# All low parts of the second attention on GpSimd, and the norms placed among the rotations

## The reference, cut to what matters

```python
xn = (x - mu) / jnp.sqrt(var + 1e-05) * ln_gamma + ln_beta      # for the attention
qkv = xn @ w_qkv                                                # [2048, 3 * 16 * 64]
qr, kr = (rotate(q), rotate(k))                                 # t1 cos - t2 sin, t2 cos + t1 sin
scores = jnp.einsum('bhid,bhjd->bhij', qr, kr) * scale
probs = jax.nn.softmax(scores, axis=-1)                         # 2048 x 2048 for each of 16 heads
out = jnp.einsum('bhij,bhjd->bhid', probs, v)
```

## Time and profile before

| | |
|---|---|
| median of 3 runs | 3486.61 us (3481.0 to 3489.35) |
| the profiled execution | 3484.36 us, its span 3482.6 us |
| busy in the span | PE 87%, PEld 37%, DVE 83%, ACT 86%, POOL 73% |
| granted TensorE clock | 0.872 of full speed |
| first attention and what precedes it | until 1866 us of the span |
| projection stage | 1866 to 2037 us |
| second attention | 2037 to 3308.4 us |
| output stage | the rest |

### The profile page before, as it was taken

How to read it: one execution, slowest core, us unless ns; L and a number is a source line. 1 busy time by engine, 2 the same in 40 slices (tenths; PEclk the granted TensorE clock), 3 DMA queues, 4 the chain that set the end, 5 groups by cost and what they waited for, 6 DMA issues and landing times. The chain is left out here.

```text
span 3482.6 us, 59948 instructions
## 1 busy us (share of the span) xinstructions
PE 3037.7 (87%) x19523; PEld 1275.8 (37%) x19523; DVE 2877.3 (83%) x4324; ACT 2989.6 (86%) x2783; POOL 2537.8 (73%) x1581
## 2 busy tenths in 40 slices
PE   6888888888888888888887968999898889989899
PEld 4222112221222212222223424555555555555547
DVE  7989999999999999999997968878887777888421
ACT  3999999999999999999996846878888888878942
POOL 5888888888888888888875524767777776767850
PEclk9788777887778777887778979999999999999999
DMA  2000000000000000000001550100000110000000
GB/s 75 6 8 7 7 0 7 7 7 7 0 7 7 7 7 0 7 7 7 3 6 40 198 143 19 32 26 26 25 26 26 44 32 26 26 26 25 20 22 13
DMA packets 59522, 85.32 MB, mean 24 GB/s; under 512 B 10065, under 2 KB 45905, under 8 KB 58961
## 3 DMA queue, kind: packets, MB, share of 16 engines
q1 hardware_dynamic: 59344, 82.93, 8.3%
HBM read 52.31 MB, written 30.54 MB: 24 GB/s over the span
## 5 line engine op out<-in xcount | busy, mean ns | idle before, releaser
L1264 POOL TENSOR_TENSOR lo<-pr,hi 128x1024 f16<-128x1024 f32 x384 | 883.1, 2323 | 396.3 <-ACT hi L1438 391.1
L1325 DVE TENSOR_REDUCE mx<-mx_ps 128x1 f32<-128x512 f32 x1024 | 660.6, 683 | 127.7 <-PE mx_ps L1480 123.9
L1453 ACT ACTIVATE pr<-s_ps 128x1024 f32<-128x1024 f32 x512 | 533.2, 1041 | 243.4 <-PE s_ps L1511 189.2
L1438 ACT ACTIVATE hi<-pr 128x1024 f16<-128x1024 f32 x512 | 549.3, 1074 | 0.0
L1480 PE MATMUL mx_ps<-ka,qa 128*128 128x512 f16 x1024 | 376.6, 397 | 128.4 <-DVE mx L1325 98.7
L722 ACT ACTIVATE wt<-wt 128x2048 f32<-128x2048 f32 x256 | 485.2, 1896 | 0.5
L713 ACT ACTIVATE wt<-wt,theta_bias 128x2048 f32<-128x2048 f32 (+2 forms) x160 | 482.4, 3015 | 3.2 <-DVE wt L563 2.7
L501 POOL TENSOR_TENSOR wt<-base,wt 128x1024 f32<-128x1024 f32 x192 | 455.3, 2371 | 16.0
L501 POOL TENSOR_TENSOR wt<-vb,wt 128x1024 f32<-128x1024 f32 x192 | 455.1, 2370 | 16.0
L1530 PE MATMUL pv_ps<-vh,hi 128*128 128x129 f16 x4096 | 434.5, 223 | 10.2 <-ACT sums L1444 3.9
L1530 PE MATMUL pv_ps<-vh,lo 128*128 128x65 f16 x4096 | 420.2, 195 | 0.0
(11 more groups left out here) (210 smaller groups left out, 5046.0 us busy)
## 6 DMA issues: line engine op xcount, KB each, us to landing
qk<-stg SPq DMA_DIRECT2D x6, 2048.0 KB, 10.6
vh<-v SPq DMA_DIRECT2D x16, 520.0 KB, 3.4
qa<-qk SPq DMA_DIRECT2D x16, 512.0 KB, 3.6
ka<-qk SPq DMA_DIRECT2D x32, 256.0 KB, 4.8
v<-v_st SPq DMA_DIRECT2D x3, 2080.0 KB, 7.9
qst<-parts_dram SPq DMA_DIRECT2D x144, 32.0 KB
kst<-parts_dram SPq DMA_DIRECT2D x144, 32.0 KB
qk<-stg SPq DMA_DIRECT2D x4, 1024.0 KB, 8.5
```

The source lines that it names most:

```text
L1264: eng.tensor_tensor(lo[:, i % NHL, :, :], pr_slot(i), hi[:, i % NHL, :, :], ALU.subtract).then_inc(lo_done, 1)
L1325: eng.tensor_reduce(mx4[:, q // NCH, q % NCH:q % NCH + 1], mx_ps[:, q % 2, :], AX.X, ALU.max)\
L1438: eng.activation(hi[:, i % NHL, :, :], pr_slot(i), ACT.Copy).then_inc(hi_done, 1)
L1453: eng.activation(pr_slot(i), s_ps[:, i % 2, :, :], ACT.Exp, scale=SM).then_inc(exp_done, 1)
```

## The change

In the attention stage the steps whose low part DVE makes go from every fourth to none (`NLV = 0`): POOL makes all 32 low parts of a head, in order, and the waits on `lo_vector` and `lo_gpsimd` are counted accordingly. DVE's two half instructions are gone. In the projection stage POOL's 16 norms no longer stand ahead of the low parts of the rotations; one stands behind the second low part of each block.

```diff
-                for k in range(NT):
-                    eng.tensor_scalar(xn[:, k, :], base[:, k, :], mv[:, k, 0:1], tmp[:, 0, k:k + 1],
-                                      ALU.subtract, ALU.mult).then_inc(xn_ready, 1)
                 for u in range(4 * NT):
...
                     eng.wait_ge(hi_ready, u + 1)
                     eng.tensor_tensor(dst[:, :, 1, :], ra[:, u % 2, :].rearrange("p (h e) -> p h e", h=HB),
                                       dst[:, :, 0, :], ALU.subtract).then_inc(lo_ready, 1)
+                    if b == 1:
+                        eng.tensor_scalar(xn[:, k, :], base[:, k, :], mv[:, k, 0:1], tmp[:, 0, k:k + 1],
+                                          ALU.subtract, ALU.mult).then_inc(xn_ready, 1)
...
-    LV = 4
+    NLV = 0
+    NLG = STEPS - NLV
...
         def on_vector(i):
-            return i % LV == LV - 1
+            return i % STEPS >= NLG
...
+            before = h + 1 + i // STEPS
             if on_vector(i):
-                eng.wait_ge(lo_vector, STEPS // LV * (h + 1) + i // LV + 1)
+                eng.wait_ge(lo_vector, NLV * before + i % STEPS - NLG + 1)
             else:
-                eng.wait_ge(lo_gpsimd, STEPS // LV * (LV - 1) * (h + 1) + i // LV * (LV - 1) + i % LV + 1)
+                eng.wait_ge(lo_gpsimd, NLG * before + i % STEPS + 1)
...
-                        for n_ in range(2):
-                            at = i - LOW - n_
-                            if (at >= 0 or not first) and on_vector(at):
-                                low_half(h, at, n_)
...
                     if last:
-                        for n_ in range(2):
-                            low_half(h, STEPS - 1, n_)
                         take(h, NS - 1)
...
-                eng.sem_inc(lo_vector, STEPS // LV)
-                eng.sem_inc(lo_gpsimd, STEPS - STEPS // LV)
+                eng.sem_inc(lo_gpsimd, NLG)
```

More of the change, by code:

```diff
@@ L1365, in take @@
                        .then_inc(attn_ready, 1)
[L1367 to L1376, removed]
                 def one(g, par, first=False, last=False):
```

## The result

The changed kernel takes 3569.99 us (median of 4 runs, 3558.07 to 3571.11) against 3483.81 of the kernel before on the same chips (4 runs, 3480.99 to 3489.35): a ratio of 1.0238, with a 95% interval of 1.0211 to 1.0264. It is slower by some 85 us; 3572 was forecast. The span of the profiled execution is 3569.3 us, 86.7 more than before.

The account below looks back on a forecast made before the run. PE sets the pace, held up by DVE. Heads 1 to 14 +94, head 0 -12, head 15 +8.4, norms -2.5: +88 on 3484.4 gives 3572 us, own range 3520 to 3610, for 8 in 10 3462 to 3610.

Parts of the forecast that it names:

- The mechanism: Second attention: a two-SBUF-input DVE instruction and a POOL low part exclude each other; multiplication 425 ns to about 2.3 us.
- the waiting one goes first: When POOL's low part ends, the waiting DVE instruction starts before POOL's next; a held addition ends 0.28 us later.
- The takes: Middle heads, steps 4, 12, 20, 28: step 4's take grows from 1.04 to 4.45 us; losses total 12.25 us a head.
- the sum: Time of a middle head: 68 + 12.25 + 3 = 83.25 us against 76.5, +6.75; for 14 heads +94.
- The undisturbed head: A middle head without DVE's half low parts and their waits: 68 us, 8.5 less than now.
- The clock: Middle heads: PE's long stops bring two slow clock stretches a head, about 1.5 us each, 3.0 us together.
- the row of maxima: Step 28: the maxima for the next head come some 1.5 us later, costing 0.5 us a head.
- Head 0: First head of the second attention, making maxima for two heads: -12 us, bounds -5 and -17.
- Head 15: Last head, without maxima: POOL's 69 us exceeds ACT's 61, low part 31 ends later; +8.4 us, bounds +5 and +10.
- The norms: Projection stage: DVE's 2.38 us wait goes, the moved norms are covered by 0.4 us of slack; net -2.5 us.
- the addition alone is held: Rival: the multiplication gets in before POOL's next low part; take 2.7 us, 3468 us in all; chance 0.13.
- takes cost little: Rival: takes hardly delay PE and POOL is the limit, 69.5 us a head, 3380 us; chance 0.08.

Follow-up runs that it names:

- the halves: The changed kernel with every low part of GpSimd split into two instructions of 128x512, without a wait between them: 3563.66 us, ratio 1.0219.
- the measured 98: The kernel before with one more multiplication, its result unused, in each take: 3587.10 us, ratio 1.0289; 98 us more, where 12 was expected.

## Why the prediction was right, point by point

- **The mechanism.** Forecast: the multiplication at about 2.3 us, the addition 1.5 to 2.3, three stops of PE a head at the banks after the takes. Measured: 2155 ns, 1560 ns, 42 waits in 14 heads. By the Trainium skill, SBUF — State Buffer, section "SBUF: two separate sides", whichever of the two starts first has the pair of SBUF ports that they share for its whole instruction, and the other is blocked. In the two timelines of step 20 the trace agrees: 2.13 and 2.11 us in place of 0.40 and 0.42. What follows on the end of that instruction the forecast had from one row: that the waiting one goes first. It held in the changed kernel and is false beside the halves (9.7 us).
- **The takes.** Forecast at step 4: 4.45 us; measured over the middle heads 3.82, at steps 12 and 20 3.95 and 4.47. The loss at step 20 is 3.95 us where the sum had 4.1. At step 4 my arithmetic had low part 3 begin on time; POOL comes out of the short steps with a backlog (ten low parts without a gap from 2155.88 us on), which moves its phase against the take, and the addition's hold varies there between 0.5 and 2.4 us in length.
- **The undisturbed head.** 68 us was too high. By the sum's own rule (a take's length less 0.4 is lost) the kernel without the division loses 1.3 + 1.8 + 1.8 = 4.9 in takes of 1.71, 2.17 and 2.21 us, so its 70.9 leave 66. This is an estimate: PE's waits at the banks in that kernel are 3.6 us a head, by which it would be 67.
- **The clock.** Two slow stretches of 1.5 us, 3.0 in all, was too low. By the same rule the takes lose 3.4 + 3.55 + 4.05 = 11.0; 66 + 11 leaves 5.7 of 82.7. One is the row of maxima: PE's wait for it is 25.4 / 14 = 1.8 us a head, where the 0.5 stood. The other 4 or so belong to the clock: 11.6 us of each head ran at half speed, against 1 in the kernel without the division. There were 37 slow stretches in 14 heads, 2.6 a head where I had taken two; 4 us are then 1.5 for each, as forecast. This is a remainder, not a measurement: no run changed the clock alone. What the sum had too high (2.0 in the undisturbed head, 0.75 in the takes) and too low (1.3 in the row, 0.9 in the clock) met, and the head came out at +6.2 against +6.75. That 3572 is within 3 us of 3570 owes something to this.
- **Head 0**: -9.4 against -12; the multiplication slipped in at two of its three takes (0.42 and 0.43 us) and was held at the third (2.23). **Head 15**: +6.4 against +8.4; low part 31 ended 7.7 us later after the head's first exp than before, and from there to the end of the last take 1.3 us were won back, where the clock had been at 0.50 and is now at 0.63.
- **The norms**: -3.1 against -2.5. The 0.4 us of cover held: DVE has no gap in the rotations, and low part 4k+2 ends before it is asked for.
- **Rivals.** That the addition alone is held, and that takes cost little, are both excluded by the multiplication's 2155 ns; the kernel without the division, 3394 us, shows about what the first would have given. It is faster than the 3468 I put on it, which kept up to one slow stretch a head and the undisturbed head of 68.

## What to carry to other kernels

A two-input instruction on VectorE between SBUF operands has to be priced with the GpSimd instruction that runs at that moment, and what counts is what stands behind it on VectorE's queue; give such small instructions to GpSimd itself, or put them where it pauses. Moving work off a loaded engine can cost more than it frees when the move closes a pause on which another pair relied. And an expectation from averages, 12 us, missed the measured 98 where a lead of 0.08 us decided who is first: read which of the two starts ahead, and by how much.

## What the runs showed of the hardware that I had not expected

- GpSimd instructions that are ready one behind the other can keep VectorE out over many instructions: an addition of 0.40 us stood for 9.7 us beside halves, a half low part 6.1 us beside full ones and the take's two instructions. In the changed kernel the same kind of instruction got in after one; without the division it did too, but for one take of 56, which stood for 6.0 us. A semaphore wait between them let VectorE in each time; what decides without it was not found.
- That wait costs GpSimd 0.28 us (2.36 from start to start against 2.08).
- Of the stops of PE, those behind takes of about 2 us, 1.2 us each without the division, left the clock at 0.99; those behind takes of about 4 us, 3.3 us each, brought it to its lower level two or three times a head (37 times in 14 heads). In the kernel before it was there 14 times, though no wait of PE for DVE was longer than 2.0 us.
